# Four head norms: the products move from GpSimd to VectorE, and the next sequence's output gate is read ahead of the gate scans

## The reference, cut to what matters

```python
x = x + 0.5 * moe(layernorm(x))
x = x + attn(layernorm(x))
x = x + 0.5 * moe(layernorm(x))

def attn(x):                                   # H = 8 heads of HD = 64
    xn = layernorm(x, ln_g, ln_b)
    x_t, r_t = xn @ W_up_l.T + b_up_l, xn @ W_up_r.T + b_up_r
    x_c = silu(causal_conv_over_features(x_t))
    x_skip, q, k = x_c @ W_skip.T + b_skip, x_c @ W_q.T + b_q, (x_c @ W_k.T + b_k) / 8
    v, o = x_t @ W_v.T + b_v, sigmoid(x_t @ W_o.T + b_o)
    i_pre, f_pre = soft_cap(x_c @ W_i.T + b_i), soft_cap(x_c @ W_f.T + b_f)
    # scan over the tokens with running maximum m, matrix state c and normalizer n
    h  = o * num / max(n . q, 1)
    hn = layernorm(h per head, mh_g, mh_b)     # the "head norm"
    return ((hn + x_skip) * silu(r_t)) @ W_down.T + b_down + x
```

## Time and profile before

| | |
|---|---|
| time of 3 runs, median (lowest to highest) | 485.36 us (484.71 to 488.89) |
| the profiled execution, its own time | 484.73 us |
| its span in the profile | 482.9 us |
| busy share of the span | TensorE 80%, VectorE 71%, ScalarE 45%, GpSimd 36% |
| mean granted TensorE clock | 0.92 of full |

### The profile page before, as it was taken

How to read it: one execution, slowest core, us unless ns; L and a number is a source line. 1 busy time by engine, 2 the same in 40 slices (tenths; PEclk the granted TensorE clock), 3 DMA queues, 4 the chain that set the end, 5 groups by cost and what they waited for, 6 DMA issues and landing times.

```text
span 482.9 us, 10042 instructions
## 1 busy us (share of the span) xinstructions
PE 386.2 (80%) x2986; PEld 323.4 (67%) x3003; DVE 342.8 (71%) x1015; ACT 216.5 (45%) x557; POOL 172.9 (36%) x158
## 2 busy tenths in 40 slices
PE   5447999906999897999898998898999983199980
PEld 5322999904777676877676777676777873199970
DVE  3692677667449979659789579789498688567763
ACT  2641344424454563545573455474555640144430
POOL 4374244521004435105433114542024317735450
PEclk9999799957999998999999999999999955589995
DMA  9992122169900000000000000000000400222216
GB/s 293 374 361 60 35 67 65 54 202 359 335 16 1 1 1 1 1 1 0 0 0 0 0 0 0 0 0 0 0 1 2 174 2 33 60 57 70 68 49 180
DMA packets 25660, 35.32 MB, mean 73 GB/s; under 512 B 3521, under 2 KB 17729, under 8 KB 25121
## 3 DMA queue, kind: packets, MB, share of 16 engines
q1 hardware_dynamic: 21554, 26.24, 16.9%
q0 software_dynamic: 2496, 5.13, 3.1%
q10 hardware_dynamic: 1584, 3.63, 2.2%
HBM read 17.52 MB, written 17.47 MB: 72 GB/s over the span
## 4 chain that ended last, share of the span: by engine, by line
PE 45%; DVE 27%; issue 10%; ACT 9%; DMA 4%; POOL 2%; SPq 1%; DVEq 1%; ACTq 0%; POOLq 0%
PE bank L856 41%; ACT WVT L749 2%; ACT E L758 2%; DVE CS L1810 2%; DMA QKT<-by_token 2%; DVE W1R L1832 1%; DVE HS L1834 1%; PE bank L973 1%; PE bank L1084 1%; DVE X L1301 1%; DVE FL L1741 1%; PE bank L877 1%; DMA by_token<-YB,IDX 1%; DVE CS L1811 1%; DVE AG L1742 1%
## 5 line engine op out<-in xcount | busy, mean ns | idle before, releaser
L519 POOL DMA_INDIRECT by_token<-YB,IDX x46 | 44.0, 957 | 58.3 <-DVE YB L1542 57.7
L856 PE MATMUL bank<-XBT,W1R 128*128 128x128 f32 x368 | 52.5, 289 | 1.1 <-DVE W1R L1530 1.0
L749 ACT ACTIVATE WVT<-bank,AC 128x128 f32<-128x128 f32 x128 | 36.6, 375 | 30.6 <-PE bank L856 30.2
L856 PEld LDWEIGHTS bank<-XBT,W1R 128*128 128x128 f32 x368 | 47.8, 203 | 2.3 <-ACT XBT L655 1.4
L856 PE MATMUL bank<-W,HT 128*128 x368 | 49.2, 277 | 0.0
L856 PEld LDWEIGHTS bank<-W,HT 128*128 128x128 f32 x368 | 45.3, 194 | 0.3
L545 POOL TENSOR_TENSOR HS<-HS,MHALF 128x8 f32<-128x8 f32 x11 | 18.1, 1643 | 70.8 <-DVE HS L1842 70.8
L713 ACT ACTIVATE QKT<-bank,COLS 128x512 f32<-128x512 f32 x32 | 22.0, 687 | 41.5 <-PE bank L856 41.5
L495 POOL DMA_INDIRECT slots<-XN,POS x32 | 31.5, 985 | 16.6 <-issue 16.6
L1796 DVE TENSOR_TENSOR WOT<-bank,WVT 128x512 f32<-128x512 f32 x32 | 21.9, 685 | 20.4 <-ACT WVT L749 20.3
L526 POOL TENSOR_TENSOR LA<-LA,MHALF 128x8 f32<-128x8 f32 x4 | 8.0, 2002 | 77.1 <-DVE LA L1688 77.1
(11 more groups left out here) (342 smaller groups left out, 1027.5 us busy)
## 6 DMA issues: line engine op xcount, KB each, us to landing
slots<-FILL SPq DMA_DIRECT2D x37, 258.0 KB, 6.2
W<-w SPq DMA_DIRECT2D x2, 2048.0 KB, 8.0
XB<-slots SPq DMA_DIRECT2D x46, 64.5 KB
W<-w SPq DMA_DIRECT2D x1, 2064.0 KB
QKT<-by_token SPq DMA_DIRECT2D x8, 256.0 KB, 4.1
slots<-QKT SPq DMA_DIRECT2D x1, 1483.5 KB, 11.2
X<-x SPq DMA_DIRECT2D x4, 256.0 KB, 5.2
out<-X SPq DMA_DIRECT2D x4, 256.0 KB, 2.5
```

What stands on the lines that cost most here:

```text
L519: g.indirect_dma_start(out=by_token[f], out_offset=bass.IndirectOffsetOnAxis(ap=IDX[:, j:j + 1], axis=0), in_=YB[:, j, :], in_offset=None) ...
L749: ins = a.activation(DT[:, hf, m, :], DM[:, m * P:(m + 1) * P], ACT.Exp, bias=AC[:, c, h:h + 1])
L856: return t_.matmul(o, l, r, start=start, stop=stop, skip_group_check=True)
```

## The change

The three products of the head norm move to VectorE for every chunk, behind `take_r` (and in chunk 1 behind `scale_norm`) and ahead of `new_state` and `gate`. GpSimd keeps the four roots of 128x8. Its addition of b_down now stands between the roots of chunks 0 and 1. And `take_r` of the next sequence's chunk 0 stands ahead of `gate_scans`, in the loop and in the opening.

```diff
@@ GpSimd
-            def head_norm(b, c):
-                n = b * NC + c
-                pool.wait_ge(hvar_ready, n + 1)
-                step.do(g.tensor_tensor(HS[:, 3, :], HS[:, 2, :], MHALF[:, 0:H], ALU.pow))
-                step.do(g.tensor_tensor(H2[:, :, :], H2[:, :, :], HS[:, 3, :].unsqueeze(2).to_broadcast([P, H, HD]), ALU.mult))
-                step.do(g.tensor_tensor(H2[:, :, :], H2[:, :, :], row("mhg", HID)..., ALU.mult))
-                pool.wait_ge(*pj_read_at(b, f"s{c}"))
-                g.tensor_tensor(H2..., H2..., SK[c], ALU.add).then_inc(hn_ready, 1)
             def sequence(b, last):
...
-                head_norm(b, 0)
-                head_norm(b, 1)
+                roots(b, 0)
                 if not last:
                     add_bdown(b + 1)
-                    head_norm(b, 2)
+                roots(b, 1)
+                if not last:
+                    roots(b, 2)
                     roots(b, 3)
                     return
@@ VectorE
             def norm_products(b, c):
-                dve.wait_ge(roots_ready, b + c - 2 if c == 3 and not (isinstance(b, int) and b == NB - 1) else b + c - 1)
+                dve.wait_ge(roots_ready, NC * b + c + 1)
@@ VectorE, chunk
                 if last and c == 3:
                     early_choice()
-                    norm_products(b, 2)
                 if c == 3 and not last:
                     low_xc(b + 1)
+                    take_r(b + 1, 0)
                     gate_scans(b + 1)
-                    take_r(b + 1, 0)
                 if more:
                     take_r(b, c + 1)
...
                 if c == 1 and not last:
                     scale_norm(b + 1)
+                if c:
+                    norm_products(b, c - 1)
                 if more:
                     new_state(b, c)
@@ VectorE, opening of sequence 0
             low_xc(0)
+            take_r(0, 0)
             gate_scans(0)
-            take_r(0, 0)
```

More of the change, by code:

```diff
@@ L539, in roots @@
                 g.tensor_tensor(HS[:, 3, :], HS[:, 2, :], MHALF[:, 0:H], ALU.pow).then_inc(roots_ready, 1)
-            def head_norm(b, c):
-                n = b * NC + c
-                pool.wait_ge(hvar_ready, n + 1)
-                step.do(g.tensor_tensor(HS[:, 3, :], HS[:, 2, :], MHALF[:, 0:H], ALU.pow))
[L546 to L549, removed]
-                pool.wait_ge(*pj_read_at(b, f"s{c}"))
-                g.tensor_tensor(H2[:, :, :].rearrange("p h d -> p (h d)"), H2[:, :, :].rearrange("p h d -> p (h d)"),
-                                SK[c], ALU.add).then_inc(hn_ready, 1)
             def sequence(b, last):
@@ L582, in _ @@
             with pool.Fori(0, NB - 1) as b:
-                step.loop(b, 3 * (NC - 1))
                 sequence(b, False)
-            step.looped(NB - 1)
             sequence(NB - 1, True)
@@ L1943, in _ @@
             weigh(0, 0, 0)
-            PER = 64
+            PER = 70
             with dve.Fori(0, NB - 1) as b:
```

## The result

The changed kernel takes 481.05 us (median of 16 runs, 479.87 to 484.64), beside 485.98 us for the kernel before in 16 runs. The ratio is 0.9908, with a 95% interval of 0.989 to 0.9925: 4.5 us or 0.9% faster by the ratio, while the two medians lie 4.9 us apart. The forecast was 481.6 us and "within 1%". The profiled execution took 481.23 us, with a span of 479.4 us.

A forecast was written before the change was run, and what follows sets the result against it. TensorE, nine tenths busy, was taken as the bound, with only its waits for VectorE, slowed by GpSimd, to regain. Loop 1.4, clock 1.4, opening 0.5 and last sequence 0.4 us took 485.36 to 481.6 us; range 478.8 to 485.6.

The forecast's parts named there:

- Chunk 1, b_down: Chunk 1 of the loop: GpSimd's b_down addition blocks one VectorE product for 0.95 us, so OUT comes 0.62 us later.
- Chunk 2: Chunk 2 of the loop: the 2.07 us of products fit into VectorE's 2.41 us of idle time and cost nothing.
- TensorE leaves chunk 2 late by 0.62 - 0.30 = 0.32 us: End of chunk 2: OUT's 0.62 us delay, less the 0.30 us that `head_x` had waited for XTL, leaves 0.32 us.
- Chunk 3: Chunk 3: scans take 1.58 us, products and their end 2.39, OUT starts 0.19 us earlier, the 2.19 us q1 wait goes.
- The new wait: Before `down_out` of chunk 2: TensorE waits about 1.4 us for ScalarE's OUTT; 0.47 us gained per looped sequence.
- Clock: First looped period: the 1.61 us lost to TensorE's lower clock after the q1 pause; about 1.4 us come back.
- Opening and last sequence: Opening: 0.5 us from q1's wait for r; last sequence, chunk 1: OUT 0.4 us earlier, carried to the chain's end.
- The sum: Whole kernel: 1.4 loop + 1.4 clock + 0.5 opening + 0.4 last sequence = 3.7 us gained.
- the clock loss stays: Rival, looped sequences: the pause is not the clock fall's whole cause; gain 2.3 us, to 483.1; chance 0.22.
- everything is hidden: Rival, loop: VectorE's chain sets the sequence through `down_out` and gets no shorter; 485 us; chance 0.12.
- VectorE becomes the bound: Rival, chunk 1 between L1697 and OUT: b_down holds up two products, OUT 2.85 us late; slower, 488.4 us; chance 0.08.
- The blocking is gone for nothing: Rival, chunk 1: the b_down addition slips in without cost; 1.42 us per looped sequence, 6.6 us in all, to 478.8; chance 0.16.

The follow-up runs named there:

- e3: Changed kernel without GpSimd's addition of b_down, which is left out of the output: 476.33 us, ratio 0.9796 to the kernel before.
- e4: The kernel before, unchanged, profiled once more to see whether the clock fall comes again: 484.68 us, one execution.
- e6: The kernel before with q3 and ScalarE's OUTT copy of chunk 2 put ahead of the squares of chunk 3: 486.18 us, ratio 1.0026.
- e9: Changed kernel with the next sequence's read of r put behind OUT of chunk 2: 482.59 us, ratio 1.0014 to the changed kernel.
- e2: Changed kernel with the read of r back behind the gate scans, in loop and opening; products stay on VectorE: 480.31 us, ratio 0.9885 to the kernel before.
- e10: Changed kernel, unchanged, profiled once more for a second look at the clock: 482.40 us, one execution.
- e7: Changed kernel with b_down added by VectorE at the end of the sequence instead of by GpSimd: 477.02 us, ratio 0.9819 to the kernel before.
- e1: The kernel before with only the read of r moved ahead of the gate scans, in loop and opening; GpSimd keeps its products: 482.08 us, ratio 0.9909.

## Why the prediction was right, point by point

The mechanism was right: the pause before q1 goes, most of it comes back as a wait at `down_out` behind the squares, and the addition of b_down blocks one product. That the time came so close (481.05 for 481.6) is in part luck. The gain of 3.7 us was too small beside 4.5 to 4.9, and the median that it was taken from, 485.36 of three runs, lay 0.6 us below that of 16 runs; the two misses partly cancel. The terms by themselves, from the profiled executions:

- **Chunk 1, b_down.** Predicted: one product blocked for 0.95 us, OUT 0.62 later. Measured: 0.95 and 0.58; e3 shows that nothing of it is hidden.
- **Chunk 2.** The products lie in TensorE's wait, as said. The step "TensorE leaves chunk 2 late by 0.62 - 0.30 = 0.32 us" was mis-sized. Measured from L1681 (L1695 before), `head_x` starts 18.03 us later in the changed kernel and 17.95 before, so it is only 0.08 late. I had taken the row's 0.30 us for all of that wait. The ends of matmuls are modelled, and in the changed kernel, where nothing waits, `head_x` starts 1.80 us after the start of a product with the values that is shown as 2.00 long. So the wait that went was worth 0.5 us.
- **Chunk 3.** Scans 1.58 us, as said. The products and their end I took as 2.39 us, from the row with 0.24 us of idle time before OUT. Measured is 2.18 (253.40 to 255.58). The two misses together are 0.45 us, and OUT of chunk 2, counted from L1681 (L1695 before), starts 0.68 us earlier instead of 0.19.
- **The new wait** at `down_out` was said to be about 1.4 us; it is 1.29. The gain per looped sequence was said to be 0.47 and is 68.83 - 67.97 = 0.86, or 2.6 us for three sequences, where the sum had 1.4. `down_out` itself starts 0.96 earlier; 0.1 of this is lost right behind it, where the product takes 1.16 us after a wait and 1.05 without one.
- **Clock.** 1.61 us in the profiled pair, said 1.4. That it goes with the pause is what the profiles of e4, e6 and e9 speak for: the kernels with a pause of about 2 us before q1 show a fall in every one of four profiles (five falls in twelve sequences, in changing places), the eight profiles without it show none in 24 sequences. If the five had fallen by chance on these 36 sequences, all would lie among the twelve about once in 480 cases. A wait of 1.3 to 1.5 us at `down_out` in six of the eight drew none. How often a fall comes in executions that were not profiled is not known, so 1.4 us for one fall fits the pair of profiles and is not shown for the medians.
- **Opening and last sequence.** 0.5 said for the opening; the first looped root comes 39.48 us after the opening's before (106.19 to 145.67) and 38.68 after it now (106.31 to 144.99), so 0.8; e2 loses the same 0.8 by the read of r alone. In the last sequence OUT of chunk 0 starts 3.57 us after the read of r instead of 3.98, the 0.4 that was said. That TensorE carries it to the end of the chain is not shown: at the last transposition of OUT (403.91 before, 398.83 now), 0.2 us are left of it. From the third looped root to there, less one period, the kernel before takes 50.1 us in its profile and 49.5 in e4, the changed one 49.9 in its profile and in e10.
- **The sum** is therefore too small at the start of the second mixture layer: TensorE's first block there starts 4.93 us earlier (422.04 to 417.11), for a predicted 3.7. The loop gives 2.6 of this, the clock 1.6 and the opening 0.8. In this profile 1.4 us are lost behind that point, where neither kernel differs. Its granted clock over the first 47 us is 0.93 where it was 0.96, and this stretch varies among the runs of one kernel: e10, with 0.93 as well, has 61.46 us from there to its end, this profile 62.29, the two of the kernel before 60.86 and 61.82. So the spans of the profiled pair differ by 3.5 us, and the measured ratio, 4.5 us, lies between 3.5 and 4.93.

Of the rivals, "the clock loss stays" and "everything is hidden" are refuted by the periods, and "VectorE becomes the bound" by one long product only. "The blocking is gone for nothing" is what e3 and e7 make true by another edit; the period is then 1.8 us below 68.83, where the rival had 1.42.

What the prediction did not see is that the two halves of the change are substitutes in the loop. I priced them together and never apart. e1 gives 68.07 us by sliding the read of r into blocked time, e2 gives 67.98 by taking the blocking away, and both together 67.97.

## What to carry to other kernels

A wait that a trace shows is worth only what lies between it and the next thing that is late on the same path: here 2.19 us of pause paid 0.86, and most of the rest stood as a new wait behind one misplaced ScalarE operation, whose place cost nothing until then (e6). After a gain, read again for the new wait, and ask whether the engine that is waited for was itself idle in front of an operation that could have stood earlier; on top of the change that reordering was worth more than the change itself (1.6 us per period beside 0.86), and without it nothing. When wide elementwise work leaves GpSimd, look for what is left of it there, since one remaining operation of 1.65 us beside VectorE cost the sequence 0.94 us. And run each half of a change by itself: here one half gave 0.75 and the other all of the 0.86 us per period.

## What the runs showed of the hardware

- One 128x512 operation on GpSimd with SBUF operands costs a two-input VectorE operation that starts beside it 0.95 us, in all three sequences. The last such cost in the loop is gone when the operation is gone (e3, 1.64 to 0.69 us), and so is one of 1.0 us in the opening (2.14 to 1.13 us). The page "SBUF — State Buffer" of the Trainium skill, section "SBUF: two separate sides", gives this as an exclusive lock; the traces agree.
- The roots of 128x8 on GpSimd, 1.64 us long, block nothing in these traces, although the same section has GpSimd's operation hold the ports for the whole instruction. Here the measurement decides. VectorE's scaling of q in chunk 3, an operation with two SBUF inputs, falls inside such a root and keeps its length:

```profile
249.03 0.69 DVE L1789 TENSOR_TENSOR QS<-QKT,E 128x512 f32<-128x512 f32 x1
```

```profile
248.46 1.64 POOL L539 TENSOR_TENSOR HS<-HS,MHALF 128x8 f32<-128x8 f32 x1 [13.01 <-DVE HS L1828]
```

- A pause of TensorE of 2.05 to 2.19 us in a program that repeats it exactly was followed by the lower clock in five of twelve cases, which cost 1.6 us each. The granted clock was 0.50 then, the lower of its two levels (1.2 GHz), and fell when q1 started or up to 1.5 us later. The same program showed it in the first sequence in one run and in the third in another, so a single profile does not tell in which sequence it comes, or how often.
